# Attention in a fused kernel: four pairs of score matmuls as one block, the values of 512 queries as one piece

## The chip, the cores and the metric

One core of one Trainium2 chip runs the whole kernel in one launch. The metric is the device time of an execution in microseconds (us). The engines work side by side, each from a queue of its own in a fixed order: TensorE (PE: matmuls; PEld: its weight loads), VectorE (DVE), ScalarE (ACT), GpSimd (POOL) and SyncE (SP, which issues DMAs). They wait for each other by semaphores.

## The reference, cut to what matters

The kernel computes four layers with a residual each: a recurrent mixer, a feed-forward layer, this attention and the feed-forward layer again, on 8 batches of 1024 tokens with 256 channels. The change touches the attention alone:

```python
def _L0_attn_b_ref(x, Wqkv, bqkv, Wout, bout):
    n_heads = 16
    qkv = (x @ Wqkv + bqkv).reshape(B, L, 3, n_heads, head_dim)      # head_dim 16, L 1024, B 8
    q, k, v = (qkv[:, :, 0], qkv[:, :, 1], qkv[:, :, 2])
    scores = jnp.einsum('bqhd,bkhd->bhqk', q, k) / math.sqrt(head_dim)
    scores = scores + slopes[None, :, None, None] * bias[None, None]  # bias: -|q - k|
    probs = jax.nn.softmax(scores, axis=-1)
    out = jnp.einsum('bhqk,bkhd->bqhd', probs, v).reshape(B, L, D)
    return out @ Wout + bout
```

## The kernel before

Heads are worked on in 32 groups g (8 batches times 4), each of four heads. A group's queries and keys are split into high and low parts and stacked on 64 partitions for each head, so that two heads lie in the two halves (row groups, rg) of TensorE's array and two such pairs of heads in two slots. The scores are computed twice. **Row scores** (`find_maxima`, line 1512) have queries on the partitions and 512 keys on the columns, into one of three places of PSUM that are handed out in turn (`misc`, a Ring over banks 5 to 7, line 1374); VectorE reduces each to its maximum (line 1731), 64 for a group. The maxima are transposed (line 1503), ScalarE copies them (lines 1642 and 1643), and they go into the query stack as a shift. **Column scores** (`attend`, line 1573) have keys on the partitions and 512 queries on the columns, in two pairs of banks; ScalarE takes the exponential of two heads at once (line 1682) into one of six buffers `p_t`. Blocks that the diagonal crosses get a short bias by two bf16 matmuls of 128 columns (line 1456). **Values** (`weigh`, line 1528): four heads' probabilities times v, each head in its own 32 columns of the array, 17 outputs (16 channels and the sum), accumulated over eight key blocks in one bank. When a half of the queries is done, ScalarE copies the bank to `pv` (line 1651), TensorE transposes it (`conclude`, line 1540), and VectorE divides (lines 1748 and 1750). After the last group of a batch, `conclude` goes on for nine steps with the output projection.

The order is written out in generators that every engine runs alike. `turns` gives for each step t (a group g, a half of 512 queries, a key block kb: 512 steps in all) four turns, pair by pair and rg by rg. In each turn TensorE issues one column matmul, one row matmul and the biases; the row scores run a group and 16 turns ahead of the column scores. `follow`, made by `tails`, is called after each pair: after pair 0 it issues the second half of the values of t-2, after pair 1 the first half of those of t-1, and one step of `conclude` where one is waiting. `side_by_side` interleaves a group's turns with the projections for queries and keys (`make_stacks`, two for each group, lines 1492 and 1493), for v (`make_values`), and the normalization. TensorE takes three kinds of waits here: for a place of `misc` (the engine that read the last user), for the exponentials (`p_made`) and for the copy of the values (`pv_made`).

A reader of the trace needs these lines: 1573 column scores, 1512 row scores, 1456 bias, 1528 values, 1540 transposes of the values, 1503 transpose of the maxima, 1731 row maximum, 1682 exponential, 1651 copy of the values.

Of the kernel before, what the change touches and what calls it, by code (L numbers as in the profile page):

```python
# [17 lines left out]
BANK = 512  # L18
# [17 lines left out]
HEADS, HD, GROUP = 16, 16, 4  # L36
GROUPS = HEADS // GROUP
QB = SEQ // P
HALVES = SEQ // BANK
# [4 lines left out]
ROWGROUPS = P // STACK  # L44
# [1261 lines left out]
def attention(nc, banks, x_in, x_out, d):  # L1306
    with nc.cleanup_on_exit(), ExitStack() as ctx:
# [3 lines left out]
        VW = HD + 1  # L1311
# [2 lines left out]
        ALL = BATCH * GROUPS  # L1314
        PAIRS = GROUP // ROWGROUPS
        PARTS = P // STACK
        WIDTH = BANK // 2
# [19 lines left out]
        half_max = sb("half_max", [P, GROUP * QB, HALVES])  # L1337
        row_max = sb("row_max", [P, 2, GROUP * QB])
        shift, shift_full = sb("shift", [2 * GROUP * QB, P], F32R), sb("shift_full", [2 * GROUP * QB, P])
        P_BUFS = 6  # L1340
        p_t = [sb(f"p_t{i}", [P, 2, BANK]) for i in range(P_BUFS)]
        pv = sb("pv", [P, BANK])
        recip = sb("recip", [P, CT * GROUP])
# [68 lines left out]
        def tails(weigh, conclude):  # L1412


            waiting = []

            def values_of(t, part):
                if t >= 0:
                    use, kb = divmod(t, QB)
                    weigh(t, use, kb, part)  # L1420
                    if kb == QB - 1 and part:
                        waiting.append(conclude(use // HALVES, use % HALVES))

            def step():
                if waiting and next(waiting[0], waiting) is waiting:
                    waiting.pop(0)

            def follow(t, pair):
                if pair == 0:
                    values_of(t - 2, 1)  # L1430
                else:
                    values_of(t - 1, 0)
                    step()

            def finish():
                end = ALL * HALVES * QB
                values_of(end - 2, 1)
                values_of(end - 1, 0)
                values_of(end - 1, 1)
                while waiting:  # L1440
                    step()

            return follow, finish

# [7 lines left out]
        def tensor(pe):  # L1452
# [65 lines left out]
                            add_block_bias(m[:, at:at + P], g, pair, rg, int(qb >= CT)).then_inc(row_scores, 1)  # L1518
                        yield

            def weigh(t, use, kb, part):
                b, hg = divmod(use // HALVES, GROUPS)
                v, cols = vs[b % 2], slice(part * WIDTH, (part + 1) * WIDTH)
                if kb == 0 and part == 0 and use:
                    pe.wait_ge(pv_made, use)
                pe.wait_ge(p_made, 2 * t + 2)
                for i in range(GROUP):
                    last = pe.matmul(values[i * SLOT:i * SLOT + VW, cols], v[:, kb, hg * GROUP + i, :],  # L1528
                                     p_t[(2 * t + i % 2) % P_BUFS][:, i // 2, cols], start=kb == 0 and part == 0, stop=kb == QB - 1 and part == 1,
                                     tile_position=(0, i * SLOT))  # L1530
                last.then_inc(weighed, 1)

# [30 lines left out]
            def attend(g, rows):  # L1563
                b = g // GROUPS
                pe.wait_ge(shift_in[g % 2], 16 * ROWGROUPS * (g // 2 + 1))
                pe.wait_ge(v_made, QB * (b + 1))
                for t, half, kb, pair, rg in turns(g):
                    first, slot = place(g, pair + rg * PAIRS)
                    stack, use = slice(first, first + STACK), 2 * t + pair
                    out, here, at = scores[use % 2][:, rg, :], kb // CT == half, kb % CT * P  # L1570
                    if use >= 2:
                        pe.wait_ge(p_made, use - 1)
                    last = pe.matmul(out, k_stack[stack, slot, kb * P:(kb + 1) * P], q_stack[stack, slot, half * BANK:(half + 1) * BANK],  # L1573
                                     start=True, stop=not here, tile_position=(first, 0))
# [21 lines left out]
        def scalar(act):  # L1596
# [13 lines left out]
            def make_values(b):  # L1610
                v = vs[b % 2]
                for i in range(QB):
                    act.wait_ge(v_ready, QB * b + i + 1)
                    if b >= 2:
                        act.wait_ge(weighed, 2 * HALVES * QB * GROUPS * (b - 1))
                    act.activation(v[:, i, :, 0:HD], by_head(misc.at["v", b, i][:, 0:DIM]), ACT.Copy).then_inc(v_made, 1)
                    yield

# [56 lines left out]
            def attend(g, rows):  # L1675
                for t, half, kb, pair, rg in turns(g):
                    if rg == ROWGROUPS - 1:
                        use = 2 * t + pair
                        act.wait_ge(col_scores, ROWGROUPS * (use + 1))
                        if use >= P_BUFS:  # L1680
                            act.wait_ge(weighed, 2 * (t - 2))
                        act.activation(p_t[use % P_BUFS][:, :, :], scores[use % 2], ACT.Exp, scale=slopes()[pair][0]).then_inc(p_made, 1)  # L1682
                    next(rows, None)
                    if rg == ROWGROUPS - 1:
                        follow(t, pair)
                    yield

            follow, finish_tails = tails(weigh, conclude)
# [6 lines left out]
        def vector(dve):  # L1695
# [39 lines left out]
            def weigh(t, use, kb, part):  # L1735
                pass

            def conclude(g, half):
# [19 lines left out]
            def attend(g, rows):  # L1758
                for t, half, kb, pair, rg in turns(g):
                    next(rows, None)  # L1760
                    if rg == ROWGROUPS - 1:
                        follow(t, pair)
                    yield

            follow, finish_tails = tails(weigh, conclude)
# [13 lines left out]
        def gpsimd(pool):  # L1779
# [45 lines left out]
            def weigh(t, use, kb, part):  # L1825
                pass

            def conclude(g, half):
# [12 lines left out]
            def attend(g, rows):  # L1841
                for t, half, kb, pair, rg in turns(g):
                    next(rows, None)
                    if rg == ROWGROUPS - 1:
                        follow(t, pair)
                    yield

            follow, finish_tails = tails(weigh, conclude)
# [13 lines left out]
        def sync(sp):  # L1862
# [50 lines left out]
            def weigh(t, use, kb, part):  # L1913
                pass

            def conclude(g, half):
# [10 lines left out]
            def attend(g, rows):  # L1927
                for t, half, kb, pair, rg in turns(g):
                    next(rows, None)
                    if rg == ROWGROUPS - 1:  # L1930
                        follow(t, pair)
                    yield

            follow, finish_tails = tails(weigh, conclude)
# [67 lines left out]
```

## Time and profile before

| | us |
|---|---|
| median of 3 runs | 3827.87 (3825.36 to 3829.14) |
| the profiled execution | 3823.22 |
| its span, first to last instruction | 3821.4 |
| TensorE busy | 3377.1 (88% of the span) |
| VectorE busy | 2690.6 (70%) |
| ScalarE busy | 2066.3 (54%) |
| column scores, from the first to the last | 1601.4 to 3408.3 |

The attention's stage takes about half of the span. The page's groups carry lines, so the stage's work can be told from that of the other layers; its times inside a step are read from the timeline. There, a row is: start in us from the span's start, duration in us, engine, line, operation, output<-input, partitions x elements, count, and in brackets the engine's idle time before it with what ended it. Matmuls in two row groups, or in four column groups, run at the same time, so durations overlap: distances between starts tell more than durations.

### The profile page before, as it was taken

The page shows a single profiled execution, that of the slowest core. Times are in us where ns is not written, and L with a number is a line of the kernel's source. Part 1 is how long each engine was busy: PE and PEld are TensorE (multiplying, and loading weights), DVE is VectorE, ACT ScalarE, POOL GpSimd, SP SyncE. Part 2 cuts the span into 40 slices and gives each one's busy share as a digit, 9 for nine tenths or more (in the row PEclk, how much of TensorE's full clock was granted, in tenths as well). Part 3 has the DMA queues.
Part 4 walks back from the last instruction along what each step waited for, and adds up shares of the span by engine and source line. Part 5 has one row for each costly group of instructions (what it writes and reads, how often), then busy time and mean ns, then how long its engine had stood idle before and what let it go on. Part 6 is the DMA issues. An engine that isn't in the chain of part 4 may idle for free. (4 is left out here: it accounts for less than half of the span.)

```text
span 3821.4 us, 87649 instructions
## 1 busy us (share of the span) xinstructions
PE 3377.1 (88%) x36196; PEld 1993.6 (52%) x36196; DVE 2690.6 (70%) x4824; ACT 2066.3 (54%) x3215; POOL 619.9 (16%) x763
## 2 busy tenths in 40 slices
PE   7888888888669993999999999999999999977998
PEld 3555555555547772444444444444444444435777
DVE  5777777777557772687776877768677786826776
ACT  2443344444335551266666666667676676664554
POOL 1211222221121222010201102011020201011212
PEclk9998898999769996699999999999999999998999
DMA  1000000000021104122222222122122121102111
GB/s 48 13 13 24 13 24 13 24 13 13 14 87 56 45 34 93 28 40 40 47 37 41 46 38 61 27 59 40 22 62 40 44 41 32 41 27 67 45 50 34
DMA packets 109901, 146.53 MB, mean 38 GB/s; under 512 B 20800, under 2 KB 93744, under 8 KB 108720
## 3 DMA queue, kind: packets, MB, share of 16 engines
q1 hardware_dynamic: 108736, 138.11, 15.3%
q8 instruction: 287, 4.70, 0.5%
q0 software_dynamic: 768, 2.82, 0.4%
q14 instruction: 110, 0.90, 0.1%
HBM read 54.15 MB, written 38.41 MB: 24 GB/s over the span
## 5 line engine op out<-in xcount | busy, mean ns | idle before, releaser
L1731 DVE TENSOR_REDUCE b_half_max<-banks 128x1 f32<-128x512 f32 x2048 | 1314.3, 685 | 444.2 <-PE banks L1456 262.7
L1682 ACT ACTIVATE b_p_t<-banks 128x1024 f32<-128x1024 f32 x1024 | 1047.0, 1025 | 397.3 <-PE banks L1456 256.0
L1512 PE MATMUL banks<-b_k_stack,b_q_stack 62*128 62x512 f32 x2048 | 829.1, 477 | 34.1 <-issue 17.8
L1573 PE MATMUL banks<-b_q_stack,b_k_stack 64*128 64x512 f32 x2048 | 851.7, 469 | 0.0
L1528 PE MATMUL banks<-b_p_t,b_v 128*17 128x256 f32 x8192 | 640.9, 385 | 25.2 <-ACT b_pv L1651 24.5
L1573 PEld LDWEIGHTS banks<-b_q_stack,b_k_stack 64*128 64x128 f32 x2048 | 342.9, 185 | 432.3 <-issue 416.8
L1456 PE MATMUL banks<-b_tables,b_halves 64*128 64x128 bf16 x4096 | 437.0, 224 | 0.0
L1512 PEld LDWEIGHTS banks<-b_k_stack,b_q_stack 62*128 62x128 f32 x2048 | 337.7, 188 | 68.7 <-issue 25.3
L1072 ACT ACTIVATE ffn_relu<-banks,ffn_scale_fc 128x512 f32<-128x512 f32 x256 | 176.2, 688 | 274.6 <-PE banks L1008 274.6
L1021 PE MATMUL banks<-ffn_proj_t,ffn_r_hi 128*128 128x256 f32 x1024 | 257.1, 285 | 2.5 <-DVE ffn_r_lo L1191 2.5
L1528 PEld LDWEIGHTS banks<-b_p_t,b_v 128*17 128x17 f32 x8192 | 135.9, 95 | 225.4 <-issue 76.9
L1022 PE MATMUL banks<-ffn_proj_t,ffn_r_lo 128*128 128x256 f32 x1024 | 251.4, 280 | 0.0
L1456 PEld LDWEIGHTS banks<-b_tables,b_halves 64*128 64x128 bf16 x4096 | 185.4, 96 | 117.3 <-issue 58.7
L1189 DVE CAST ffn_r_hi<-ffn_square 128x512 fp32r<-128x512 f32 x256 | 131.1, 512 | 163.5 <-ACT ffn_square L1076 163.2
L1006 PE MATMUL banks<-ffn_x_hi,ffn_fc_t 128*128 128x512 f32 x512 | 208.9, 408 | 34.1 <-DVE ffn_low L1179 34.1
L1007 PE MATMUL banks<-ffn_x_lo,ffn_fc_t 128*128 128x512 f32 x512 | 205.0, 400 | 0.0
L1021 PEld LDWEIGHTS banks<-ffn_proj_t,ffn_r_hi 128*128 128x128 f32 x1024 | 194.3, 190 | 12.2 <-DVE ffn_r_lo L1191 2.9
L1022 PEld LDWEIGHTS banks<-ffn_proj_t,ffn_r_lo 128*128 128x128 f32 x1024 | 193.0, 188 | 8.1
L1191 DVE TENSOR_TENSOR ffn_r_lo<-ffn_square,ffn_r_hi 128x512 fp32r<-128x512 f32 x256 | 188.9, 738 | 8.8
L1813 POOL TENSOR_TENSOR b_qk_lo<-b_qk,b_qk_hi 128x512 fp32r<-128x512 f32 x64 | 81.6, 1276 | 657.4 <-ACT b_qk L1631 500.0
L268 PE MATMUL banks<-a_z,a_w_x 128*128 128x512 f32 x320 | 171.6, 657 | 16.3 <-ACT a_gate_low L450 12.8
L1076 ACT ACTIVATE ffn_square<-ffn_relu 128x512 f32<-128x512 f32 x256 | 161.8, 632 | 8.7 <-DVE ffn_r_lo L1191 0.6
(235 smaller groups left out, 4994.6 us busy)
## 6 DMA issues: line engine op xcount, KB each, us to landing
ffn_x<-x SPq DMA_DIRECT2D x32, 512.0 KB, 3.9
b_q_stack<-b_qk_hi SPq DMA_DIRECT2D x256, 64.0 KB
b_k_stack<-b_qk_hi SPq DMA_DIRECT2D x256, 64.0 KB
a_x<-hidden_states SPq DMA_DIRECT2D x16, 512.0 KB, 3.4
x<-a_x SPq DMA_DIRECT2D x16, 512.0 KB, 3.4
x<-ffn_x SPq DMA_DIRECT2D x16, 512.0 KB, 2.9
b_x<-x SPq DMA_DIRECT2D x8, 1024.0 KB, 6.7
b_k_stack<-b_qk_lo SPq DMA_DIRECT2D x128, 64.0 KB
```

The source lines that it names most:

```text
L1006: pe.matmul(b, fc_t[:, kt, cols], x_hi[:, kt, :], start=kt == 0, stop=False)
L1007: pe.matmul(b, fc_t[:, kt, cols], x_lo[:, kt, :], start=False, stop=False)
L1021: pe.matmul(b[:, 0:DIM], r_hi[par][:, m, i * P:(i + 1) * P], proj_t[:, m, :], start=m == 0, stop=False)
L1022: last = pe.matmul(b[:, 0:DIM], r_lo[par][:, m, i * P:(i + 1) * P], proj_t[:, m, :], start=False, stop=m == HT - 1)
L1072: act.activation(relu[use % 2][:, :], high[use % 3], ACT.Relu, scale=scale_fc[:, m:m + 1]).then_inc(relu_made, 1)
L1191: dve.tensor_tensor(r_lo[par][:, m, :], square[use % 2][:, :], r_hi[par][:, m, :].bitcast(F32), ALU.subtract).then_inc(r_lo_made, 1)
L1456: last = pe.matmul(out, halves[rows, part, :], tables[rows, g % GROUPS * PAIRS + pair, variant, part, :], start=False, stop=part == PARTS ...
L1512: last = pe.matmul(m, q_stack[rows, slot, qb * P:(qb + 1) * P], k_stack[rows, slot, half * BANK:(half + 1) * BANK], start=True, stop=not h ...
L1528: last = pe.matmul(values[i * SLOT:i * SLOT + VW, cols], v[:, kb, hg * GROUP + i, :], p_t[(2 * t + i % 2) % P_BUFS][:, i // 2, cols], star ...
L1573: last = pe.matmul(out, k_stack[stack, slot, kb * P:(kb + 1) * P], q_stack[stack, slot, half * BANK:(half + 1) * BANK], start=True, stop=n ...
L1682: act.activation(p_t[use % P_BUFS][:, :, :], scores[use % 2], ACT.Exp, scale=slopes()[pair][0]).then_inc(p_made, 1)
L1731: dve.tensor_reduce(half_max[:, (pair + rg * PAIRS) * QB + qb, half:half + 1], misc.at["max", g, turn], axis=AX.X, op=ALU.max, negate=True ...
```

## The change

`follow` is called once for each step, after all its four turns, instead of after each pair. It issues the values of t-1 for all 512 queries in one piece (four heads, 512 columns each, one `weighed` for each step instead of two), and then at once one step of `conclude`, where one is waiting. The buffers for probabilities go from six to four. Nothing else changes: the same scores, the same exponentials, the same places for row scores.

```diff
-        P_BUFS = 6
+        P_BUFS = 4
...
-            def values_of(t, part):
+            def values_of(t):
                 if t >= 0:
                     use, kb = divmod(t, QB)
-                    weigh(t, use, kb, part)
-                    if kb == QB - 1 and part:
+                    weigh(t, use, kb)
+                    if kb == QB - 1:
                         waiting.append(conclude(use // HALVES, use % HALVES))
 
-            def step():
+            def follow(t):
+                values_of(t - 1)
                 if waiting and next(waiting[0], waiting) is waiting:
                     waiting.pop(0)
 
-            def follow(t, pair):
-                if pair == 0:
-                    values_of(t - 2, 1)
-                else:
-                    values_of(t - 1, 0)
-                    step()
-
...
-            def weigh(t, use, kb, part):
+            def weigh(t, use, kb):
                 b, hg = divmod(use // HALVES, GROUPS)
-                v, cols = vs[b % 2], slice(part * WIDTH, (part + 1) * WIDTH)
-                if kb == 0 and part == 0 and use:
+                v = vs[b % 2]
+                if kb == 0 and use:
                     pe.wait_ge(pv_made, use)
                 pe.wait_ge(p_made, 2 * t + 2)
                 for i in range(GROUP):
-                    last = pe.matmul(values[i * SLOT:i * SLOT + VW, cols], v[:, kb, hg * GROUP + i, :],
-                                     p_t[(2 * t + i % 2) % P_BUFS][:, i // 2, cols], start=kb == 0 and part == 0, stop=kb == QB - 1 and part == 1,
+                    last = pe.matmul(values[i * SLOT:i * SLOT + VW, :], v[:, kb, hg * GROUP + i, :],
+                                     p_t[(2 * t + i % 2) % P_BUFS][:, i // 2, :], start=kb == 0, stop=kb == QB - 1,
                                      tile_position=(0, i * SLOT))
                 last.then_inc(weighed, 1)
...
-                    if rg == ROWGROUPS - 1:
-                        follow(t, pair)
+                    if (pair, rg) == (PAIRS - 1, ROWGROUPS - 1):
+                        follow(t)
...
-            def weigh(t, use, kb, part):
-                if kb == QB - 1 and part:
-                    act.wait_ge(weighed, 2 * (t + 1))
+            def weigh(t, use, kb):
+                if kb == QB - 1:
+                    act.wait_ge(weighed, t + 1)
                     if use:
                         act.wait_ge(pv_turned, use)
                     act.activation(pv[:, :], values, ACT.Copy).then_inc(pv_made, 1)
...
                         if use >= P_BUFS:
-                            act.wait_ge(weighed, 2 * (t - 2))
+                            act.wait_ge(weighed, t - P_BUFS // 2 + 1)
```

The same two lines of `attend` change on ScalarE, VectorE, GpSimd and SyncE, whose `follow` moves in the same way.

## Rows read from the trace of the kernel before

**Rows 1.** The page: granted TensorE clock, span in 40 equal slices, in tenths.
```profile
PEclk9998898999769996699999999999999999998999
```

**Rows 2.** Busy us of each engine in a stretch, granted clock, DMA share, GB/s.
```profile
1610.00:3410.00 1800.00, 1752.40 (x17364) 855.28 (x17364) 1327.77 (x2231) 1232.86 (x1461) 217.74 (x280) 1.00 0.21 40
```

**Rows 3.** The page's groups: count | busy us, mean ns | idle before, releaser.
```profile
L1731 DVE TENSOR_REDUCE b_half_max<-banks 128x1 f32<-128x512 f32 x2048 | 1314.3, 685 | 444.2 <-PE banks L1456 262.7 <-PE banks L1512 155.7
L1682 ACT ACTIVATE b_p_t<-banks 128x1024 f32<-128x1024 f32 x1024 | 1047.0, 1025 | 397.3 <-PE banks L1456 256.0
```

**Rows 4.** Timeline, 2192.7 to 2198.9: values, and values two groups on, no column bias.
```profile
2193.58 0.63 PE L1528 MATMUL banks<-b_p_t,b_v 128*17 128x256 f32 x8
...
2196.20 0.63 PE L1528 MATMUL banks<-b_p_t,b_v 128*17 128x256 f32 x8
```

**Rows 5.** Timeline of PE, 2116.8 to 2120: the same with bias on all columns.
```profile
2117.03 0.63 PE L1528 MATMUL banks<-b_p_t,b_v 128*17 128x256 f32 x8
...
2119.96 0.41 PE L1528 MATMUL banks<-b_p_t,b_v 128*17 128x256 f32 x4
```

**Rows 6.** Timeline: row matmul and its reduce, with bias and without.
```profile
2174.00 0.49 PE L1512 MATMUL banks<-b_k_stack,b_q_stack 62*128 62x512 f32 x1
...
2174.69 0.69 DVE L1731 TENSOR_REDUCE b_half_max<-banks 128x1 f32<-128x512 f32 x1 [0.27 <-PE banks L1456]
...
2177.99 0.49 PE L1512 MATMUL banks<-b_k_stack,b_q_stack 62*128 62x512 f32 x1
...
2178.54 0.69 DVE L1731 TENSOR_REDUCE b_half_max<-banks 128x1 f32<-128x512 f32 x1 [1.78 <-PE banks L1512]
```

**Rows 7.** Timeline, 1575 to 1580, row scores alone.
```profile
1574.71 5.49 DVE L1731 TENSOR_REDUCE b_half_max<-banks 128x1 f32<-128x512 f32 x9 [2.27 <-PE banks L1456]
1575.45 0.28 PEld L1512 LDWEIGHTS banks<-b_k_stack,b_q_stack 62*128 62x128 f32 x1 [0.76 <-DVE b_half_max L1731]
```

**Rows 8.** Timeline of PE, 3376 to 3384: column scores and values, no rows.
```profile
3382.22 0.51 PE L1573 MATMUL banks<-b_q_stack,b_k_stack 64*128 64x512 f32 x2
...
3382.79 0.63 PE L1528 MATMUL banks<-b_p_t,b_v 128*17 128x256 f32 x8
3383.34 0.50 PE L1573 MATMUL banks<-b_q_stack,b_k_stack 64*128 64x512 f32 x2
3383.78 0.41 PE L1528 MATMUL banks<-b_p_t,b_v 128*17 128x256 f32 x4
```

**Rows 9.** Timeline: two passes of 512 fp32 columns.
```profile
2177.04 1.02 PE L1493 MATMUL banks<-b_xn_t,b_w_qk 128*128 128x512 f32 x2
```

**Rows 10.** Timeline of PE, 2151 to 2154: values, transposes, next scores, middle of g.
```profile
2151.76 0.63 PE L1528 MATMUL banks<-b_p_t,b_v 128*17 128x256 f32 x8 [0.20 <-ACT b_pv L1651]
2152.32 0.66 PE L1540 MATMUL banks<-b_ident,b_pv 128*128 128x128 f32 x4
2152.91 0.50 PE L1573 MATMUL banks<-b_q_stack,b_k_stack 64*128 64x512 f32 x1
...
2153.25 0.39 PE L1573 MATMUL banks<-b_q_stack,b_k_stack 64*128 64x512 f32 x1
```

**Rows 11.** Timeline, 2178 to 2183: the edge of g.
```profile
2178.78 0.77 ACT L1631 ACTIVATE b_qk<-banks,b_b_scaled,b_scale_qk 128x512 f32<-128x512 f32 x1
...
2180.34 0.61 ACT L1651 ACTIVATE b_pv<-banks 128x512 f32<-128x512 f32 x1
...
2182.15 0.49 PE L1573 MATMUL banks<-b_q_stack,b_k_stack 64*128 64x512 f32 x1
```

**Rows 12.** Timeline, 2189 to 2193: the block behind the second projection.
```profile
2189.91 0.50 PE L1573 MATMUL banks<-b_q_stack,b_k_stack 64*128 64x512 f32 x1
...
2192.74 0.49 PE L1573 MATMUL banks<-b_q_stack,b_k_stack 64*128 64x512 f32 x1
```

**Rows 13.** Timeline of PE, 2162 to 2164: column and row score around the shift's copies.
```profile
2162.29 0.49 PE L1573 MATMUL banks<-b_q_stack,b_k_stack 64*128 64x512 f32 x1
2163.23 0.50 PE L1512 MATMUL banks<-b_k_stack,b_q_stack 62*128 62x512 f32 x1 [0.45 <-ACT b_shift_full L1643]
```

More of the change, by code:

```diff
@@ L1316, in attention @@
         PARTS = P // STACK
-        WIDTH = BANK // 2
         ident, halves = sb("ident", [P, P]), sb("halves", [P, PARTS, P], BF16)
@@ L1415, in tails @@
             waiting = []
-            def values_of(t, part):
+            def values_of(t):
                 if t >= 0:
                     use, kb = divmod(t, QB)
-                    weigh(t, use, kb, part)
-                    if kb == QB - 1 and part:
+                    weigh(t, use, kb)
+                    if kb == QB - 1:
                         waiting.append(conclude(use // HALVES, use % HALVES))
-            def step():
+            def follow(t):
+                values_of(t - 1)
                 if waiting and next(waiting[0], waiting) is waiting:
                     waiting.pop(0)
-            def follow(t, pair):
-                if pair == 0:
-                    values_of(t - 2, 1)
-                else:
-                    values_of(t - 1, 0)
-                    step()
             def finish():
                 end = ALL * HALVES * QB
-                values_of(end - 2, 1)
-                values_of(end - 1, 0)
-                values_of(end - 1, 1)
+                follow(end)
                 while waiting:
-                    step()
+                    follow(0)
             return follow, finish
@@ L1614, in make_values @@
                     if b >= 2:
-                        act.wait_ge(weighed, 2 * HALVES * QB * GROUPS * (b - 1))
+                        act.wait_ge(weighed, HALVES * QB * GROUPS * (b - 1))
                     act.activation(v[:, i, :, 0:HD], by_head(misc.at["v", b, i][:, 0:DIM]), ACT.Copy).then_inc(v_made, 1)
@@ L1680, in attend @@
                         if use >= P_BUFS:
-                            act.wait_ge(weighed, 2 * (t - 2))
+                            act.wait_ge(weighed, t - P_BUFS // 2 + 1)
                         act.activation(p_t[use % P_BUFS][:, :, :], scores[use % 2], ACT.Exp, scale=slopes()[pair][0]).then_inc(p_made, 1)
                     next(rows, None)
-                    if rg == ROWGROUPS - 1:
-                        follow(t, pair)
+                    if (pair, rg) == (PAIRS - 1, ROWGROUPS - 1):
+                        follow(t)
                     yield
@@ L1733, in find_maxima, with weigh @@
                     yield
-            def weigh(t, use, kb, part):
+            def weigh(t, use, kb):
                 pass
@@ L1760, in attend @@
                     next(rows, None)
-                    if rg == ROWGROUPS - 1:
-                        follow(t, pair)
+                    if (pair, rg) == (PAIRS - 1, ROWGROUPS - 1):
+                        follow(t)
                     yield
@@ L1823, in find_maxima, with weigh @@
                     yield
-            def weigh(t, use, kb, part):
+            def weigh(t, use, kb):
                 pass
@@ L1843, in attend @@
                     next(rows, None)
-                    if rg == ROWGROUPS - 1:
-                        follow(t, pair)
+                    if (pair, rg) == (PAIRS - 1, ROWGROUPS - 1):
+                        follow(t)
                     yield
@@ L1911, in find_maxima, with weigh @@
                     yield
-            def weigh(t, use, kb, part):
+            def weigh(t, use, kb):
                 pass
@@ L1929, in attend @@
                     next(rows, None)
-                    if rg == ROWGROUPS - 1:
-                        follow(t, pair)
+                    if (pair, rg) == (PAIRS - 1, ROWGROUPS - 1):
+                        follow(t)
                     yield
```

## The prediction, made before the changed kernel was seen

> **What bounds the kernel now.** I read the page's slices first. The stage that the diff touches lies where the slices show TensorE's clock granted in full, from the 18th to the 36th [rows 1]. The table by stretch gives, for the 1800 us from 1610 to 3410, TensorE busy 1752, ScalarE 1233, VectorE 1328 [rows 2]: TensorE sets the pace, VectorE has a quarter to spare. Next I read the groups [rows 3]: 2048 row reduces of 685 ns and 1024 exponentials of 1025 ns. Then the timeline, because the change is about order. A block is one step t: four column matmuls, four row matmuls, two groups of values. Without bias on the columns it lasts 2.62 us from values to values two groups on [rows 4], with bias on all columns 2.93 [rows 5]; half of the 512 blocks are of either kind, mean 2.775. Everything in it is in TensorE's order, and it hardly ever waits.
>
> What the timeline also shows is how row scores reach VectorE. The reduce of an unbiased row starts 0.55 us after the row's matmul (2177.99, 2178.54), of a biased one 0.69 after (2174.00, 2174.69) [rows 6]. Before the first block, where there are only row scores, each row matmul starts 0.05 after the end of the reduce three rows earlier: there TensorE waits for one of the three places of the ring, and VectorE goes on every 0.60 (9 reduces in 5.49) [rows 7]. In the blocks of today that wait doesn't bind, as a group of values lies between rows 2 and 3, and another between rows 4 and 5.
>
> **The change, part by part.**
> (1) Values in one piece. Two groups of 256 columns become one of 512. From a group of values to the next scores passes 0.55 [rows 8]. An fp32 pass over 512 columns takes 0.43 (two in 1.02 less the 0.59 of one) [rows 9], so one over 256 some 0.21, and the group of 512, with two passes as now, lasts 0.55 + 0.43 = 0.98. Two groups took 1.10: 0.12 less a block. Joining pair 2 to pair 3 saves a little more, as pair 3 no longer follows values.
> (2) Four rows in a row. The fourth row matmul now needs the place of the first, and nothing but scores lies between. It can start no sooner than latency + reduce + release after the first: 0.55 + 0.69 + 0.05 = 1.29 where row 1 has no bias, 0.69 + 0.69 + 0.05 = 1.43 where it has one. Unheld it would start at about 0.8 to 1.2. Behind it on TensorE stand the values and everything else. From a score matmul that starts alone to the values passes 0.44 without bias and 0.57 with [rows 8]. In each block the row bias falls on rows 1 and 2 or on rows 3 and 4. So the new block is 1.43 + 0.44 + 0.98 = 2.85 or 1.29 + 0.57 + 0.98 = 2.84, with or without column bias: I take 2.845. Against 2.775 that is +0.07; the blocks without column bias lose 0.22, those with it win 0.085. Some 461 of the 512 are plain in this sense (less 32 with a query/key projection inside, below, and 19 at the end that have no rows): 461 x 0.07 = **+32 us**. Bounds: the held row's tail may be shorter by 0.1 (values after the last score of a half block, not after one that starts alone), or longer by 0.1: 2.75 to 2.95, -12 to +81 us.
> (3) Turning the values, 64 times. The step that transposes pv now stands right behind the last values of a half, in the same call of follow; before, a group of values and a pair of scores lay between. TensorE must wait for ScalarE's copy: the group's last pass ends 0.63 + 0.43 = 1.06 after its start [rows 8, 9], copy 0.61 [rows 11], release 0.05 [rows 7], so transposes at 1.72 and the next pair 0.59 later [rows 10], at 2.31 in place of 0.98: +1.33. Before it cost 0.59 for the transposes and a wait of the next values for the same copy, 0.20 in the middle of g [rows 10], which goes, since the new copy is made a block ahead of its user. Middle of g: 1.33 - 0.79 = +0.54, x 32 = **+17**.
> (4) At the edge of g the copy stood behind two copies of the projection, so that from the pair at 2177.99 [rows 6] to the one at 2182.15 passed 4.16 [rows 11]. Now pv's copy is ahead of them, but row 4 of that block needs a place that the second of these copies frees (2179.55, 1.56 after the pair, so row at 1.61): 1.61 + 0.57 + 0.98 = 3.16, plus the 1.33 of (3): 4.49, +0.33 x 31 = **+10**.
> (5) The other projection stands ahead of a block and takes a place, so the block's third row waits for its copies: 1.61 + 0.34 + 0.44 + 0.98 = 3.37 against 2.845; before, that block took 2.83 [rows 12], 0.21 over its kind. +0.315 x 32 = **+10**.
> (6) Shift of g. The row after the maxima's transpose waits 0.94 (2162.29 to 2163.23 [rows 13]) for two copies that ScalarE makes behind an exponential. The longer values cover 0.43 of it, and the transpose falls into time for which row 4 would be held anyway. Between -0.43 and -1.2; I take -0.8, x 31 = **-25**.
> (7) The 19 last blocks have no rows and no hold: 0.12 to 0.3 each, **-4**.
> (8) At nothing: four p_t buffers for six. Exponentials of t need the values of t-2, which TensorE issues ahead of block t. The second exponential of a block ends by about 3.1 (first ready at about 0.8 to 1.1, then two of 1.02 [rows 3]), needed by pair 3 of the next block at 3.4: its cover is 0.3, and what goes beyond it is paid in full. VectorE's reciprocal and product after the transposes lie in the 1.1 us before the next row is ready. What SP and GpSimd do in the tails (the store of x, the two additions) moves by half a block, and nobody waits for it.
>
> Sum: 32 + 17 + 10 + 10 - 25 - 4 = **+40 us**. The profiled execution took 3823.22 (1.8 around its span of 3821.4), so 3863; the median of the runs shown is 4.65 above that execution, so I forecast **3868**.
>
> Two rules of the Trainium skill bear on this. TensorEngine Tiling (Array Packing), Key Properties, says that changing the tiling mode drains TensorE; the trace agrees so far that scores follow values only after 0.55. By it each removed switch is a gain, which is the first rival below. The same page, PSUM Bottleneck, says that tiling speeds up TensorE but not the evacuation of PSUM, which may become the bottleneck. By that rule the rows of a block wait for VectorE, as in (2); rows 7 show such a wait where only rows run.
>
> **The rivals.**
> A, faster: the packing pays in full. Place: rows 3 and 4 of a block. It decides if row 1's place is free by the time row 4 comes unheld. Then pairs 2 to 4 follow at 0.34 [rows 10], 0.24 and 0.24, values at 0.33 and 0.98: 2.13, with the biases some 2.45 in the mean, -0.325 x 461 = -150, the rest +8: 3686. The 0.24 is an estimate, 0.34 less the 0.11 by which the matmul that starts alone lasts longer (0.50 against 0.39 [rows 10]). Against it: latency and reduce, 1.24, are both measured.
> B, even: the hold costs what the joined values save. A block of 2.76 and the special places at 0 to +8: 3820 to 3835. It decides if the held row's values follow 0.08 sooner.
> C, a small gain: as B, with blocks near 2.73 (the lower bound) and the shift at its best: 3800 to 3820.
> D, worse: the cover of (8) fails. ScalarE also copies pv, v and the projections; once the second exponential is late, columns of pair 3 wait, rows behind them, and each next block inherits it. +0.2 on every block: 3970. For it: only 0.3 of cover; against it: ScalarE is idle for 567 us of the 1800 [rows 2].
> That the change does nothing of what it says can't be: the order is written out.
>
> **How the numbers follow.** Forecast 0.62 (its own range 3836 to 3930), B 0.13, C 0.10, A 0.07, D 0.08. A measurement tells about 0.2% from no change, some 7.7 us. Faster 0.17 (A, C), same 0.13 (B), slower 0.70. The range for 8 in 10: from 3805, within C, to 3930, the upper bound of (2).
>
> **What would show it.** The changed profile should have row matmuls with idle time ended by the row reduce, about once a block; in the timeline row 4 starts 0.05 after the first reduce's end; blocks of about 2.85 of both kinds; TensorE's busy share in the stage well below 97%, since waits replace passes; the 64 transposes behind an idle ended by pv's copy, and none ahead of values; the shift's wait below 0.5. Wrong I am if blocks without column bias stay at 2.6 or below (then row 4 isn't held as I say), or if exponentials end the waits of the columns (D).

## The result, and the profile after

The changed kernel takes 3899.5 us (median of 4 runs, 3892.5 to 3901.8) against 3827.4 for the kernel before on the same chip: a ratio of 1.0185, with a 95% interval from 1.0168 to 1.0203. It is 72 us slower; the forecast was +40, 3868, with a range from 3805 to 3930. The profiled execution took 3901.8.

The page of the changed kernel, its head and the groups that answer to [rows 1, 3]. The columns of a group are count | busy us, mean ns | idle before, releaser:

```profile
span 3900.0 us, 79459 instructions
...
PEclk9988998899679996799999999999999999998999
...
L1722 DVE TENSOR_REDUCE b_half_max<-banks 128x1 f32<-128x512 f32 x2048 | 1282.5, 684 | 505.1 <-PE banks L1447 307.6
L1673 ACT ACTIVATE b_p_t<-banks 128x1024 f32<-128x1024 f32 x1024 | 1003.3, 1023 | 391.5 <-PE banks L1447 221.6
...
L1564 PE MATMUL banks<-b_q_stack,b_k_stack 64*128 64x512 f32 x2048 | 763.6, 455 | 1.4 <-ACT b_p_t L1673 1.1
...
L1519 PE MATMUL banks<-b_p_t,b_v 128*17 128x512 f32 x4096 | 541.0, 600 | 0.6 <-ACT b_p_t L1673 0.6
...
L1503 PEld LDWEIGHTS banks<-b_k_stack,b_q_stack 62*128 62x128 f32 x2048 | 355.3, 188 | 201.5 <-DVE b_half_max L1722 116.2
```

Line numbers are nine lower than before: 1722 is the row maximum, 1673 the exponential, 1519 the values, 1503 the row scores, 1564 the column scores, 1531 the transposes of pv, 1642 the copy of the values. The last group is the one that changed most: the weight loads of row scores stood idle for 202 us, 116 of them until a row maximum. The page of the kernel before has for the same group 69 us, and no row maximum as the main cause:

```profile
L1512 PEld LDWEIGHTS banks<-b_k_stack,b_q_stack 62*128 62x128 f32 x2048 | 337.7, 188 | 68.7 <-issue 25.3
```

The first two groups have the same work as [rows 3]. The row maximum has more idle time before it (505 us for 444), the exponential a little less (391.5 for 397.3).

The stage, in the tables by stretch of the kernel before and of the changed one (busy us of PE, PEld, DVE, ACT and POOL, then granted clock, DMA share, GB/s):

```profile
1601.86:3422.78 1820.92, 1770.96 (x17472) 868.42 (x17470) 1333.74 (x2241) 1241.65 (x1481) 224.15 (x290) 1.00 0.20 40
```

```profile
1611.44:3501.87 1890.43, 1797.64 (x13375) 848.93 (x13374) 1303.78 (x2241) 1215.12 (x1481) 224.79 (x290) 1.00 0.20 38
```

From the first column score to the end of the stage 1820.9 us became 1890.4: 69.5 of the 72 lie here. Ahead of it the two profiled executions differ by 9.6 (1601.9 and 1611.4), in layers that the change doesn't touch. That start varies among all thirteen profiled executions of this case, from 1597.6 to 1611.4, with the kernels mixed, so I compare stages: the time from the first column score to the last, 1806.4 before (1601.9 to 3408.3) and 1875.4 after (1611.4 to 3486.9).

What a plain block looks like now. The timeline of the changed kernel, one without bias on the columns:

```profile
2226.57 0.49 PE L1564 MATMUL banks<-b_q_stack,b_k_stack 64*128 64x512 f32 x1
...
2226.58 0.73 PE L1503 MATMUL banks<-b_k_stack,b_q_stack 62*128 62x512 f32 x2
...
2227.23 2.48 DVE L1722 TENSOR_REDUCE b_half_max<-banks 128x1 f32<-128x512 f32 x4 [0.49 <-PE banks L1447]
2227.25 0.48 PE L1564 MATMUL banks<-b_q_stack,b_k_stack 64*128 64x512 f32 x1
2227.32 0.40 PE L1503 MATMUL banks<-b_k_stack,b_q_stack 62*128 62x512 f32 x1
...
2227.57 0.40 PE L1564 MATMUL banks<-b_q_stack,b_k_stack 64*128 64x512 f32 x1
...
2227.98 0.18 PEld L1503 LDWEIGHTS banks<-b_k_stack,b_q_stack 62*128 62x128 f32 x1 [0.47 <-DVE b_half_max L1722]
...
2228.40 1.05 PE L1519 MATMUL banks<-b_p_t,b_v 128*17 128x512 f32 x8
...
2229.39 0.50 PE L1564 MATMUL banks<-b_q_stack,b_k_stack 64*128 64x512 f32 x1
```

Row 1 starts at 2226.58, its reduce at 2227.23 (0.65 later, it has a bias) and ends 0.69 after, at 2227.92; row 4 starts at 2227.98, 0.06 behind. Three rows and four columns were started within 1.0 us (2226.57 to 2227.57); then the fourth row waits, and the values behind it: 0.42 from row 4 to the values, 0.99 from there to the next block. The block is 2.82 us. In the kernel before, one of this kind took 2.62 [rows 4].

### The profile page after: what moved, and what is told of

It reads as the page before. It is cut to its first block and busy times, and to the rows that moved or that the text cites. A ratio compares the mean times of both kernels' runs of the same rounds, so it can differ in the third digit from the quotient of the medians.

```text
span 3900.0 us, 79459 instructions
## 1 busy us (share of the span) xinstructions
PE 3412.0 (87%) x32100; PEld 1979.9 (51%) x32100; DVE 2660.7 (68%) x4824; ACT 2039.4 (52%) x3215; POOL 620.5 (16%) x763
## 3 DMA queue, kind: packets, MB, share of 16 engines
q0 software_dynamic: 768, 2.82, 0.4%
## 5 line engine op out<-in xcount | busy, mean ns | idle before, releaser
L1722 DVE TENSOR_REDUCE b_half_max<-banks 128x1 f32<-128x512 f32 x2048 | 1282.5, 684 | 505.1 <-PE banks L1447 307.6
L1673 ACT ACTIVATE b_p_t<-banks 128x1024 f32<-128x1024 f32 x1024 | 1003.3, 1023 | 391.5 <-PE banks L1447 221.6
L1503 PE MATMUL banks<-b_k_stack,b_q_stack 62*128 62x512 f32 x2048 | 852.3, 480 | 53.8 <-ACT b_qk L1622 19.3
L1564 PE MATMUL banks<-b_q_stack,b_k_stack 64*128 64x512 f32 x2048 | 763.6, 455 | 1.4 <-ACT b_p_t L1673 1.1
L1519 PE MATMUL banks<-b_p_t,b_v 128*17 128x512 f32 x4096 | 541.0, 600 | 0.6 <-ACT b_p_t L1673 0.6
L1447 PE MATMUL banks<-b_tables,b_halves 64*128 64x128 bf16 x4096 | 468.2, 224 | 0.0
L1503 PEld LDWEIGHTS banks<-b_k_stack,b_q_stack 62*128 62x128 f32 x2048 | 355.3, 188 | 201.5 <-DVE b_half_max L1722 116.2
L1447 PEld LDWEIGHTS banks<-b_tables,b_halves 64*128 64x128 bf16 x4096 | 197.5, 96 | 140.4 <-issue 89.2
L508 ACT ACTIVATE a_pair<-banks 32x128 f32<-32x128 f32 x64 | 17.1, 267 | 263.2 <-DVE a_masked L658 263.2
```

The costliest lines, as they stand in the source:

```text
L1447: last = pe.matmul(out, halves[rows, part, :], tables[rows, g % GROUPS * PAIRS + pair, variant, part, :], start=False, stop=part == PARTS ...
L1503: last = pe.matmul(m, q_stack[rows, slot, qb * P:(qb + 1) * P], k_stack[rows, slot, half * BANK:(half + 1) * BANK], start=True, stop=not h ...
L1519: last = pe.matmul(values[i * SLOT:i * SLOT + VW, :], v[:, kb, hg * GROUP + i, :], p_t[(2 * t + i % 2) % P_BUFS][:, i // 2, :], start=kb = ...
L1722: dve.tensor_reduce(half_max[:, (pair + rg * PAIRS) * QB + qb, half:half + 1], misc.at["max", g, turn], axis=AX.X, op=ALU.max, negate=True ...
```

## The experiments

Each kernel was timed in three rounds beside the kernel before, on one chip for each batch of runs. The ratio is to the kernel before, with its 95% interval; "stage" is the time from the first column score to the last in the profiled execution.

| kernel | median us | ratio | stage us |
|---|---|---|---|
| before | 3823 to 3827 | 1 | 1806.4 |
| changed | 3899.5 | 1.0185 (1.0168 to 1.0203) | 1875.4 |
| short_max | 3777.6 | 0.9881 (0.9864 to 0.9898) | 1764.6 |
| short_max_before | 3813.4 | 0.9977 (0.9965 to 0.9989) | 1805.0 |
| turn_later | 3863.6 | 1.0109 (1.0094 to 1.0124) | 1846.0 |
| turn_later_rest_behind | 3844.9 | 1.0053 (1.0032 to 1.0073) | 1822.1 |
| short_max_turn_later | 3722.1 | 0.9723 (0.9701 to 0.9745) | 1716.0 |
| two_pieces | 3893.6 | 1.0190 (1.0168 to 1.0212) | 1879.3 |
| six_buffers | 3897.3 | 1.0185 (1.0168 to 1.0202) | 1875.4 |
| shift_first | 3800.6 | 0.9929 (0.9912 to 0.9946) | 1777.9 |
| shift_first_stacks_later | 3836.5 | 1.0030 (1.0012 to 1.0048) | 1813.3 |
| shift_first_stacks_6_17 | 3783.7 | 0.9891 (0.9874 to 0.9909) | 1762.1 |
| changed_all_three | 3828.2 | 1.0007 (0.9994 to 1.0020) | 1809.1 |

**Is the fourth row held by the first reduce? A shorter reduce, in the changed kernel and in the one before.** The theory is that of term 2; the rival, that TensorE's own work sets the block. The row maximum leaves out every second column, so these two kernels don't compute the reference.

```diff
-   dve.tensor_reduce(half_max[...], misc.at["max", g, turn],
+   dve.tensor_reduce(half_max[...], misc.at["max", g, turn].rearrange("p (n s) -> p n s", s=2)[:, :, 0],
```

> The changed kernel, but the row maximum reads every second column of a row alone (256 of 512; the other columns are left out of the maximum), so that a reduce is some 0.27 us shorter, an estimate from 685 ns for 512. If the fourth row is held by the first reduce, the hold falls from 1.29 and 1.43 to 1.02 and 1.16, and plain blocks from 2.82 and 2.85 to about 2.60: 90 to 125 us less than the changed kernel (3775 to 3810). Rival: VectorE has a quarter to spare and TensorE's own work sets the block, then 0 to 15 us.

> The kernel before with the same short row maximum (every second column left out of the maximum): the control. Its blocks aren't held, so I expect 0 to 10 us less than 3827. If row reduces paced that kernel too, it would gain as much as the changed one, 90 us or more.

Measured: 3777.6, 122 us less than the changed kernel; its stage 111 shorter. The reduce fell from 684 to 421 ns. The timeline of short_max, a plain block of the same kind:

```profile
2176.30 0.73 PE L1503 MATMUL banks<-b_k_stack,b_q_stack 62*128 62x512 f32 x2
...
2176.96 1.43 DVE L1722 TENSOR_REDUCE b_half_max<-banks 128x1 f32<-128x256 f32 x4 [1.02 <-PE banks L1447]
...
2177.44 0.18 PEld L1503 LDWEIGHTS banks<-b_k_stack,b_q_stack 62*128 62x128 f32 x1 [0.20 <-DVE b_half_max L1722]
...
2177.86 1.05 PE L1519 MATMUL banks<-b_p_t,b_v 128*17 128x512 f32 x8
...
2178.85 0.50 PE L1564 MATMUL banks<-b_q_stack,b_k_stack 64*128 64x512 f32 x1
```

Row 4 now starts 1.14 after row 1 instead of 1.40, and the block is 2.55 instead of 2.82: the 0.26 that the reduce lost, in full. Blocks with column bias fell a little less, from 2.86 to 2.65: in their timeline row 4 starts 0.14 after the first reduce's end and no wait stands before it, so there TensorE's own work sets the block. In those without column bias row 4 still waits (0.20 in the line above). The control's stage fell by 1.4 us and its blocks of this kind stayed at 2.62 (its median is 10 us lower, most of which the stage doesn't show). So the same 0.26 us is worth 111 us behind the change and next to nothing ahead of it. Against its own control, short_max's stage is 40 us shorter. The hold is shown, with its size, and so is that the change made it. VectorE has still more than a quarter of the stage idle; it is the latency of one reduce, not its throughput, that binds.

**What do the transposes cost behind the last values?** In turn_later the step of `conclude` is taken ahead of the values.

```diff
 def follow(t):
-    values_of(t - 1)
     if waiting and next(waiting[0], waiting) is waiting:
         waiting.pop(0)
+    values_of(t - 1)
```

> The changed kernel, but follow takes its step of conclude ahead of the values, so that the transposes of a half come one block after its last values, when pv has long been copied. My theory (term 3 of the sum, in the changed trace 4.27 us for a block that ends in transposes against 2.85 for one that doesn't, so 1.41, of which the transposes themselves are 0.59): 63 x 0.82 = 52 us less than the changed kernel, about 3847. Rival: the wait for ScalarE's copy only moves to the exponentials behind it, and less than 15 us come back (3885 or more).

Measured: 3863.6, 36 us less, not 52. The changed kernel's timeline shows the wait that is gone in it:

```profile
2236.89 1.05 PE L1519 MATMUL banks<-b_p_t,b_v 128*17 128x512 f32 x8
2238.01 0.60 ACT L1642 ACTIVATE b_pv<-banks 128x512 f32<-128x512 f32 x1 [0.28 <-PE banks L1519]
2238.75 0.63 PE L1531 MATMUL banks<-b_ident,b_pv 128*128 128x128 f32 x4 [0.81 <-ACT b_pv L1642]
2239.31 0.50 PE L1564 MATMUL banks<-b_q_stack,b_k_stack 64*128 64x512 f32 x1
```

From the values to the next scores 2.42 us, where a plain block has 0.99. In turn_later no such wait is left, and a block with transposes takes 3.48 against 2.86 without. But the steps of the output projection moved ahead of the values too, and there they meet the reduces. The timeline of turn_later:

```profile
2097.55 0.18 PEld L1503 LDWEIGHTS banks<-b_k_stack,b_q_stack 62*128 62x128 f32 x1 [0.43 <-DVE b_half_max L1722]
...
2098.15 0.20 PEld L1542 LDWEIGHTS banks<-b_ident,b_att 128*128 128x128 f32 x2 [0.42 <-DVE b_half_max L1722]
...
2098.75 0.30 PEld L1550 LDWEIGHTS banks<-b_w_out,b_att_t 128*128 128x128 f32 x2 [0.39 <-DVE b_half_max L1722]
```

Each takes a place of the same ring, and each place is freed by a reduce 0.6 us after the last. Such a block took 4.65 us, against 4.05 in the changed kernel, where these steps stand behind the long values and don't wait for a reduce. turn_later_rest_behind moves the transposes alone (the first step of a `conclude` ahead of the values, the later ones behind, and none in the call that issues a half's last values; the loop at the end, not shown, is changed to match):

```diff
+    first = waiting and t % QB == 1
+    if first and next(waiting[0], waiting) is waiting:
+        waiting.pop(0)
     values_of(t - 1)
-    if waiting and next(waiting[0], waiting) is waiting:
+    if not first and t % QB and waiting and next(waiting[0], waiting) is waiting:
         waiting.pop(0)
```

> turn_later, but only the transposes of a half go ahead of the values; the steps of the output projection stay behind them, as in the changed kernel. turn_later came to 3864 where I expected 3847, and in its trace the blocks with such a step took 4.65 us against 4.05 in the changed kernel, 0.6 more, some 60 times: 36 us. If that is where the rest went: 3825 to 3835, about the kernel before. Rival: the 0.6 belongs to the later transposes themselves, then 3855 to 3865 again.

Measured: 3844.9, above the 3825 to 3835 expected. The stage is 53 us shorter than the changed kernel's, what I had expected of turn_later, but only 24 us shorter than turn_later's. I had counted 60 steps at 0.6; the groups that carry the output projection came down by 3.4 us each (67.2 to 63.8), which is about six steps for each of seven batches. The blocks with such a step fell from 4.65 to 4.06. So the place of the transposes is worth 53 us of the stage, and 16 remain over the kernel before. Not all of the 53 is loss against the kernel before: blocks 0 and 1 of a group now take 9.02 together, where that kernel took 9.55, and this gain of some 16 us pays for part of the held rows.

**Both suspects gone.**

> The changed kernel with the short row maximum (every second column left out of the maximum) and the transposes one block later. By my theory both suspects are gone and the packing shows: 3725 to 3760, well below the kernel before. If the two share a cost, less than the sum of both alone. Rival A's 3686 would be reached only if nothing else held the rows.

Measured: 3722.1, stage 1716.0, a little below the range. The two more than add up: alone they took 110.9 and 29.5 from the stage, together 159.4, 19 more than the sum. Blocks with a step of the output projection account for it: 3.85 where turn_later has 4.65. Of those 0.80, a plain block loses 0.26; the rest, over some 40 of them, is about 20 us. Plain blocks are 2.55 and 2.65 as in short_max. Rival A's 3686 supposed nothing that holds a row, and 1.14 us of latency and short reduce still do.

**What is one piece worth?** two_pieces keeps the new order and cuts the values into two groups of 256 columns, one behind the other.

```diff
-    for i in range(GROUP):
-        last = pe.matmul(values[i * SLOT:i * SLOT + VW, :], v[:, kb, hg * GROUP + i, :], p_t[...][:, i // 2, :], ...
+    for part in range(2):
+        cols = slice(part * BANK // 2, (part + 1) * BANK // 2)
+        for i in range(GROUP):
+            last = pe.matmul(values[i * SLOT:i * SLOT + VW, cols], v[:, kb, hg * GROUP + i, :], p_t[...][:, i // 2, cols], ...
```

> The changed kernel's order, but the values of a block in two groups of 256 columns, one right behind the other, as the kernel before has them but together. If the fixed cost of a group lies in the switch between scores and values, the second group costs only 0.03 a block: +15 us over the changed kernel (3915). If each group has a fixed cost of its own, as term 1 of my sum took it (0.12 a block): +61 us (3960).

Measured: a stage 3.8 us longer than the changed kernel's; part of that is one more stretch at the lower clock (last section). A group of 16 blocks with nothing else in it is 0.1 us longer (54.88 for 54.78), 0.006 a block. The medians (3893.6 and 3899.5) can't be told apart. Its timeline:

```profile
2229.85 1.06 PE L1521 MATMUL banks<-b_p_t,b_v 128*17 128x256 f32 x16
2230.84 0.50 PE L1566 MATMUL banks<-b_q_stack,b_k_stack 64*128 64x512 f32 x1
```

Sixteen matmuls of 256 columns take from 2229.85 to the next scores at 2230.84, 0.99, as eight of 512 do. So the 0.12 a block that one piece saves isn't in the width of the matmul: what a group of values costs beside its columns is the turn from scores to values and back, and one turn less is in the order, which two_pieces keeps. Half as many instructions are worth nothing here.

**Are four buffers enough?** P_BUFS is 6 again in the changed kernel.

> The changed kernel with six buffers for probabilities, as before. My theory (part 8): the four buffers cost nothing, within 4 us of the changed kernel. Rival: exponentials wait for the values of two steps back, then 20 us or more come back.

Measured: 3897.3, stage 1875.4 in both. They are.

**Two waits of the kernel before.** Its trace had waits that the change shrank by accident: 0.94 for the shift's copies [rows 13], and the one at the edge of a group behind the projection's copies [rows 11]. These experiments take them away in the kernel before, where the change isn't. First, ScalarE copies the maxima ahead of the exponential of that turn:

```diff
 for t, half, kb, pair, rg in turns(g):
+    next(rows, None)
     if rg == ROWGROUPS - 1:
         ... act.activation(p_t[...], scores[use % 2], ACT.Exp, ...).then_inc(p_made, 1)
-    next(rows, None)
```

> The kernel before, with one thing moved: on ScalarE the two copies of the transposed maxima (lines 1642 and 1643) come ahead of the exponential of their turn instead of behind it, so that the row after them has its place 1 us sooner. Before, it waited 0.94 us, 31 times. I expect 20 to 29 us less than 3827. Rival: the exponential, 0.4 us later, holds the columns instead, and 10 us or less are gained.

Measured: 3800.6, and the stage 28.5 us shorter. The timeline of shift_first, where the row of [rows 13] isn't held any more:

```profile
2208.77 0.26 ACT L1643 ACTIVATE b_shift_full<-banks 64x128 f32<-64x128 f32 x1
...
2209.38 1.02 ACT L1683 ACTIVATE b_p_t<-banks 128x1024 f32<-128x1024 f32 x1 [0.35 <-PE banks L1456]
...
2209.82 0.50 PE L1573 MATMUL banks<-b_q_stack,b_k_stack 64*128 64x512 f32 x1
...
2209.83 0.50 PE L1512 MATMUL banks<-b_k_stack,b_q_stack 62*128 62x512 f32 x1
```

Second, the projections come later, by the weight of `make_stacks` in `schedule`: 2 (turns 8 and 24) and 2.75 (turns 6 and 17) for 3 (turns 5 and 16).

```diff
-    *([(STACKS, stacks(g + 2), 3)] if 0 <= g + 2 < ALL else []),
+    *([(STACKS, stacks(g + 2), 2.75)] if 0 <= g + 2 < ALL else []),
```

> As shift_first, and the two projections of a group are spread at turns 8 and 24 instead of 5 and 16 (their weight in the schedule 2 for 3), so that pv's copy at the edge of a group no longer stands behind the projection's two copies. The wait of the values there was 0.93 (0.27 in the middle of a group): 0.65 x 31 = 20 us on top of shift_first, about 3780. Rival: the projection's copies hold other rows or columns at their new turns, and nothing is gained on top.

Measured: 3836.5, 36 us more than shift_first, a miss. Its timeline says part of why: at turns 8 and 24 the stacks' DMAs are late for the first row of the next group but one.

```profile
2218.49 0.50 PE L1512 MATMUL banks<-b_k_stack,b_q_stack 62*128 62x512 f32 x1 [1.33 <-DMA b_k_stack<-b_k_bias]
```

TensorE waited so 13 times, 14 us in all, of the 35 by which the stage is longer than shift_first's. The rest isn't split up: rows also waited for the row maximum behind the statistics of the normalization (seven times, 1.5 to 2.1 us), and nine stretches of the stage, 48 us together, ran at 1.2 GHz, where shift_first's stage has none.

> As shift_first_stacks_later, but the projections only one turn later than before (weight 2.75: turns 6 and 17 for 5 and 16), so that pv's copy at the edge of a group is just ahead of the projection's copies, and the stacks are still there in time. In the run with turns 8 and 24, blocks 12 (4.59 us against 3.72) paid back what block 1 had won. I expect block 1 to lose most of its 0.93 wait and block 12 to stay at 3.72: 20 to 29 us below shift_first, 3772 to 3781. Rival: the stacks come late here too, no gain.

Measured: 3783.7, 17 us less than shift_first (stage 15.8 less), somewhat short of the 20 to 29 expected. Block 1 of a group (block 0 being its first step) fell from 6.63 to 5.51, though not in the seven groups with a normalization, and block 12 stayed at 3.52, but the second projection, now within block 4, gave back 0.32: blocks 3 and 4 took 7.99 together for 7.67. Groups with a normalization gained nothing (54.06 us, now 54.25), the others 0.6 to 0.8. It is the fastest kernel that computes the reference: 1.1% below the kernel before, about 3% below the changed one.

> The changed kernel with the transposes alone one block later, the shift's copies ahead of the exponential, and the projections at turns 6 and 17. By my theory what is left of the change is the held fourth row (+0.20 in blocks without column bias, -0.08 in those with it, 0.06 in the mean, 30 us): 25 to 40 us above shift_first_stacks_6_17, 3800 to 3815. Rival: once its special blocks are mended the packing wins, and it comes out below that kernel.

Measured: 3828.2, above the 3800 to 3815 expected and the kernel before to within its interval. Its stage is 47 us longer than that of shift_first_stacks_6_17, more than the 25 to 40 expected. Both have the two repairs; what lies between them is the change without its worst term, and it loses. The packing doesn't win by itself.

## Why the prediction was right, and where it was off

The mechanism, the sign and most terms held, the sum was too low: +40 forecast, +72 measured, 69 of them in the stage. Block lengths below go from first column score to first column score; they are medians over the seven groups in which nothing else is made (g = 2, 6, ... 26). "Plain" is the difference of plain blocks, which term 2 has already.

| term | forecast us | measured us | from |
|---|---|---|---|
| (2) the held row, 461 plain blocks | +32 | +33 | 248 without column bias 2.62 to 2.82, 213 with it 2.93 to 2.85 |
| (3) transposes, middle of a group | +17 | +25 | blocks 8 and 9: 6.11 to 7.31, less 0.41 plain |
| (4) transposes, edge of a group | +10 | +13 | blocks 0 and 1: 9.55 to 9.88, plus 0.08 plain |
| (5) the other projection | +10 | +6 | blocks 3 and 4: 7.67 to 7.99, less 0.12 plain |
| (6) the shift | -25 | -11 | blocks 12 and 13: 7.39 to 6.90, plus 0.16 plain |
| (7) the last blocks | -4 | -1 | no gain in those without bias |
| statistics of the normalization | not in the sum | +12 | seven batches, 1.1 (four) or 2.4 (three) more than the other groups |

Together +77 where the stage shows 69. The table counts all groups alike, and they aren't. A group with nothing else in it lost 2.15 us (52.63 to 54.78). The seven that also make the values of the next batch lost 1.65 (61.12 to 62.77), and the seven that carry the output projection 1.3 (62.95 to 64.26). That is some 9 us less than the table has for them.

The steps of the sum that failed are (3), by 8 us, and (6), by 14, and the statistics, some 12, which stood at nothing. In (2) I took half of the 461 blocks for each kind. It is 248 without column bias and 213 with it, and with these counts my own block of 2.845 gives +38. So that the 32 comes so near the measured 33 is in part luck.

- (1) and (2). The held row is right in cause, kind and roughly in size: release 0.06 after the reduce (0.05 said), blocks of one length whatever the bias (2.82 and 2.85 for 2.845), a loss where there is no column bias and a win where there is. short_max shows the cause. What (1) said of the joined values came out in its number, 0.12, but two_pieces shows where that is: in one turn less between scores and values, and nothing in the longer matmul.
- (3) was mis-sized. I had the transposes 1.72 after the values; the trace has 1.86 (2236.89, 2238.75), since between the copy's end and their start lie 0.14 and not the 0.05 of a row, and the copy starts 0.07 after the values' end. The rest is a cover that I named and thought safe: VectorE's reciprocal and product, in "the 1.1 us before the next row is ready". They end at 2240.13, and the next block's first reduce starts 0.73 after its row instead of 0.55, so its row 4 is held 0.16 longer: 3.02 where a plain one has 2.85. turn_later_rest_behind shows the price of the place, 53 us of the stage.
- (4) and (5) were right in mechanism. In (5) the row behind the projection waits for its copy as said.
- (6) was wrong in size. The wait itself did nearly as I said: 0.56 in the changed kernel (2251.56 to 2252.12 below) for 0.94, so 0.38 of the 0.43 are there. What failed is "the transpose falls into time for which row 4 would be held anyway": the block of the transpose takes 3.52, as before. The timeline of the changed kernel:

```profile
2248.81 2.57 DVE L1722 TENSOR_REDUCE b_half_max<-banks 128x1 f32<-128x512 f32 x4 [0.31 <-PE banks L1447]
...
2249.30 0.30 PE L1494 MATMUL banks<-b_ident,b_row_max 128*64 128x128 f32 x1
2249.56 0.50 PE L1503 MATMUL banks<-b_k_stack,b_q_stack 62*128 62x512 f32 x1
...
2250.15 0.49 PE L1503 MATMUL banks<-b_k_stack,b_q_stack 62*128 62x512 f32 x1
...
2250.72 1.02 ACT L1673 ACTIVATE b_p_t<-banks 128x1024 f32<-128x1024 f32 x1 [0.58 <-PE banks L1447]
2251.56 0.50 PE L1564 MATMUL banks<-b_q_stack,b_k_stack 64*128 64x512 f32 x1
2251.64 0.26 ACT L1633 ACTIVATE b_shift<-banks 64x128 fp32r<-64x128 f32 x1
2251.80 0.26 ACT L1634 ACTIVATE b_shift_full<-banks 64x128 f32<-64x128 f32 x1
...
2252.12 0.50 PE L1503 MATMUL banks<-b_k_stack,b_q_stack 62*128 62x512 f32 x1
```

  The transpose (L1494) takes a place of the ring for itself. So already row 3 waits for the first reduce (2248.81 + 0.69 = 2249.50, row at 2249.56), and row 4 for the second, which comes 0.60 later (row at 2250.15). So nearly the whole cost of the transpose is there again, as one more turn of the reduce. ScalarE idles 0.58 before the exponential behind the held rows, and the shift's copies come behind that exponential.
- What I left out: once in a batch VectorE makes the statistics of the normalization (2151.29 to 2154.67). Before, they fell beside the projection's matmuls, and block 1 took as long with them as without (6.63). Now the late reciprocal and product lie ahead of them (to 2151.38), the row behind the projection waits, and block 1 takes 6.70 with them and 5.61 without. The timeline of the changed kernel, first VectorE and then the row:

```profile
2151.29 2.70 DVE L1693 BATCH_NORM_STATS2 b_stats<-b_x 128x6 f32<-128x256 f32 x8
2154.03 0.64 DVE L1697 BATCH_NORM_AGGREGATE b_mean_var<-b_stats 128x2 f32<-128x6 f32 x8
2154.59 2.67 DVE L1722 TENSOR_REDUCE b_half_max<-banks 128x1 f32<-128x512 f32 x4
```

```profile
2155.30 0.50 PE L1503 MATMUL banks<-b_k_stack,b_q_stack 62*128 62x512 f32 x1 [1.54 <-DVE b_half_max L1722]
```

- (8): the buffers cost nothing (six_buffers). Rival D didn't come true either: TensorE itself stood idle for an exponential before column scores for 1.1 us in the whole execution (the group of line 1564 above). Weight loads of column scores are listed with 0.85 of idle time ended by an exponential, but that time lies under the values, and it is 0.85 too where the view names no releaser.
- Of what I said the profile would show, two things failed. The shift's wait is 0.56, not below 0.5. And TensorE's busy share in the stage is 95.1% (1797.6 of 1890.4), not well below 97. While one row group's matmul is held, the other row group's still runs (in the plain block above from 2227.57 to 2227.97, row 4 starting at 2227.98), and its time counts as busy. The idle time of the weight loads of row scores told the hold, the busy share didn't.

Rival A, 3686, would have needed rows that nothing holds. Its gain is there: three rows and four columns started within 1.0 us, and two_pieces shows that it is the turn that costs. With full reduces the gain is lost behind a place of PSUM, with short ones part of it appears: short_max is 46 us below the kernel before, and 36 below its control. The Trainium skill has a rule for either side: changing the tiling mode drains TensorE (TensorEngine Tiling (Array Packing), Key Properties). And tiling doesn't speed up the evacuation of PSUM, which may become the bottleneck (the Trainium skill, the same page, PSUM Bottleneck). The traces agree with both: one turn less saves 0.12 us a block, and the held row costs more than that where there is no column bias (2.62 to 2.82).

## What to carry to other kernels

Before you pack one engine's work into a burst, count how many results of the burst the buffers between it and the next engine can hold. The first result beyond that number can start no sooner than the latency plus one evacuation after the first of the burst (here the fourth row, 1.3 to 1.4 us), however idle the other engine is on average. A wait that a step takes on work issued just ahead of it costs its whole round trip (here TensorE stood idle 0.8 us for ScalarE's copy, 64 times); put one independent block between. And look for the waits that a change removes by accident: taken by themselves, two of them gave 1.1%.

## What the runs showed of the hardware that I had not expected

Two groups of values in the same column tiles, one behind the other, cost no more than one of double width: 0.99 us for both, 0.006 a block between them.

In the stage the granted clock of the kernel before was 1.00 throughout, the full 2.4 GHz. In the changed kernel three of the seven waits behind the statistics were followed by a stretch at half of it, 1.2 instead of 2.4 GHz. The table by stretch of the changed kernel, columns as in that of the stage, for the one behind 2155.30:

```profile
2156.70:2160.11 3.41, 3.41 (x24) 1.86 (x16) 1.97 (x4) 1.40 (x2) 2.64 (x4) 0.50 0.00 0
```

Matmuls of the row scores took 0.79 there for 0.50. It cost 1.3 us each time, the difference between the 2.4 and the 1.1 in the table's last row. Why the third, fifth and seventh and not the others stays open: all seven waits are 1.84 us long by the idle time of their weight loads. It isn't the place in the kernel, for in six_buffers it was the third, fifth and sixth.
